# Cross attention: the context tile turned and split earlier in each step

## What is computed

```python
Q = (x @ Wq.T).reshape(B, xN, 16, 32)
KV = (z @ Wkv.T).reshape(B, zN, 2, 16, 32)
K = KV[:, :, 0]
V = KV[:, :, 1]
attn = jnp.einsum('bqhd,bkhd->bhqk', Q, K) * SCALE
attn = jax.nn.softmax(attn, axis=-1)
O = jnp.einsum('bhqk,bkhd->bqhd', attn, V).reshape(B, xN, 512)
return O @ Wo.T
```

## Time and profile before

| | |
|---|---|
| runs | 1499.83, 1495.79, 1500.88 us |
| median | 1499.83 us |
| span of the profiled execution | 1492.9 us |
| PE, PEld busy | 96%, 86% |
| DVE, ACT, POOL busy | 73%, 54%, 36% |

### The profile page before, as it was taken

The page is one execution under the profiler, slowest core; times in us unless marked ns, Lnnn a source line. Parts: engine busy times, 40 slices in busy tenths (PEclk is TensorE's granted clock), DMA queues, the critical chain, the costliest instruction groups (busy, mean ns, idle before and its releaser), DMA issues. The chain is left out here.

```text
span 1492.9 us, 39481 instructions
## 1 busy us (share of the span) xinstructions
PE 1434.5 (96%) x14944; PEld 1281.3 (86%) x14944; DVE 1088.6 (73%) x1945; ACT 807.5 (54%) x1525; POOL 543.6 (36%) x810
## 2 busy tenths in 40 slices
PE   7999999999999999998999998799999999999998
PEld 6888888988888888887778786698999999999997
DVE  3676777767777677776667686797887878787785
ACT  4666666666666666654434434345555545555452
POOL 1222222221222222224866876453333333333232
PEclk9999999999999999999999999899999999999999
DMA  6301101000001100100011014179877878787871
GB/s 239 125 28 31 30 22 29 29 22 29 22 28 28 29 28 23 30 9 1 31 38 38 32 38 155 57 220 314 281 263 247 286 253 267 262 279 238 292 256 44
DMA packets 130734, 174.11 MB, mean 117 GB/s; under 512 B 16953, under 2 KB 89337, under 8 KB 130626
## 3 DMA queue, kind: packets, MB, share of 16 engines
q1 hardware_dynamic: 120242, 145.56, 30.1%
q0 software_dynamic: 10384, 27.05, 5.0%
HBM read 157.18 MB, written 19.06 MB: 118 GB/s over the span
## 5 line engine op out<-in xcount | busy, mean ns | idle before, releaser
L2229 DVE TENSOR_TENSOR split<-raw,split 128x1024 fp32r<-128x1024 f32 x204 | 242.3, 1220 | 7.2 <-ACT split L2169 6.0
L52 PE MATMUL bank<-split_xT,split 128*128 128x256 f32 x768 | 216.5, 282 | 0.4 <-DVE split L2229 0.2
L54 PE MATMUL bank<-split_xT,split 128*128 128x256 f32 x768 | 215.4, 281 | 0.0
L53 PE MATMUL bank<-split_xT,split 128*128 128x256 f32 x768 | 215.4, 280 | 0.0
L2169 ACT CAST split<-raw 128x1024 fp32r<-128x1024 f32 x202 | 203.2, 1048 | 6.9 <-DMA raw<-in_L_ffn_W_dram 3.2
L596 ACT ACTIVATE Pr<-xa_s,nmax 128x257 f32<-128x257 f32 x256 | 118.7, 473 | 124.9 <-DVE nmax L696 124.8
L2189 ACT ACTIVATE sl<-bank 128x256 f32<-128x256 f32 x115 | 44.2, 384 | 240.8 <-PE bank L54 223.5
L52 PE MATMUL xa_s<-split,split 128*128 128x258 f32 x512 | 150.5, 294 | 1.9 <-DVE split L628 1.9
L52 PEld LDWEIGHTS bank<-split_xT,split 128*128 128x128 f32 x768 | 144.9, 189 | 7.0 <-issue 2.8
L53 PEld LDWEIGHTS bank<-split_xT,split 128*128 128x128 f32 x768 | 145.0, 189 | 3.1
L53 PE MATMUL xa_s<-split,split 128*128 128x258 f32 x512 | 145.6, 284 | 0.0
(11 more groups left out here) (317 smaller groups left out, 3915.1 us busy)
## 6 DMA issues: line engine op xcount, KB each, us to landing
raw<-in_L_ffn_W_dram SPq DMA_DIRECT2D x207, 512.0 KB
raw<-in_ctx_dram SPq DMA_DIRECT2D x64, 256.0 KB, 2.6
out_dram<-x_res SPq DMA_DIRECT2D x16, 256.0 KB
xs<-xn SPq DMA_DIRECT2D x16, 256.0 KB
x_res<-in_x_dram SPq DMA_DIRECT2D x1, 3584.0 KB, 18.7
VL<-v_last_rows SPq DMA_DIRECT2D x128, 2.0 KB, 1.5
raw_o<-in_L_xattn_Wo_dram SPq DMA_DIRECT2D x1, 1024.0 KB, 6.4
raw_q<-in_L_xattn_Wq_dram SPq DMA_DIRECT2D x1, 1024.0 KB, 9.5
```

Source lines behind the costliest of these rows:

```text
L52: pe.matmul(out, lh, rh, start=start, stop=False)
L53: pe.matmul(out, ll, rh, start=False, stop=False)
L54: return pe.matmul(out, lh, rl, start=False, stop=stop)
L2229: vW.done(dve.tensor_tensor(lo, raw, hi.bitcast(F32), ALU.subtract), f"p{c}{q}")
```

## The change

Three calls move, one on each of three engines, and nothing is added or removed. On PE `turn_z` of the next step stands right behind the scores (and behind `turn_last`), ahead of the gather. On ACT `z_hi` stands between the second and the third exponential. On DVE `z_lo` stands behind the second maximum (and `last_rows`, `normalise`), ahead of the reciprocal.

```diff
                             turn_last(i - 1)
+                        if not (last and j == BT - 1):
+                            turn_z(s + 1, (j + 1) % BT, i + (j + 1) // BT)
                         if first and j == 1:
                             pe.wait_ge(vl_split, 2)
...
                             turn_x(pe, i + 2)
-                        if not (last and j == BT - 1):
-                            turn_z(s + 1, (j + 1) % BT, i + (j + 1) // BT)
...
                         for m in range(NQ):
+                            if m == 2 and not (last and j == BT - 1):
+                                z_hi(s + 1)
                             act.wait_ge(v_mx, 2 * s + m // 2 + 1)
...
                             x_out(act, i + 2)
-                        if not (last and j == BT - 1):
-                            z_hi(s + 1)
...
                             normalise(dve, i + 2)
+                        if not (last and j == BT - 1):
+                            z_lo(s + 1)
                         dve.wait_ge(a_E, 4 * s + 4)
                         dve.reciprocal(rinv[:], rsum[:]).then_inc(v_R, 1)
...
                             qk_lo(s + 1, u if j < BT - 1 else 1 - u, (j + 1) % BT)
-                            z_lo(s + 1)
```

## The result

| | kernel before | changed kernel |
|---|---|---|
| median of 20 runs each | 1497.1 us (1492.4 to 1500.9) | 1500.95 us (1497.7 to 1504.0) |
| ratio | | 1.0025, 95% interval 1.0016 to 1.0034 |
| span of the profiled execution | 1492.9 us | 1500.4 us |

The change costs 3.8 us where -0.1 was forecast. The median of the kernel before is 2.7 us lower here than in the three runs shown ahead of the prediction. The 1501 us of the changed kernel lie inside the range, and 0.25% is inside the 0.3% that had the chance of 0.77, but only because both were wide: the loss is clear of the measurement, and in the loop, where it begins, I had put it at none. The prediction was wrong.

The account below looks back on a forecast made before the run. PE's own chain was taken to bound the kernel. The terms -0.4 - 0.4 - 0.1 + 0.2 + 0.6 + 0 in the loop gave -0.1 us, a median of 1499.7 us, with the range 1495.0 to 1504.0.

Parts of the forecast that it names:

- the cost of the transposes' move: PE: the gather starts 0.44 us later and ends where the four transposes ended before, sum zero.
- the border before `absorb_k`: PE at j = 0: a 512-wide matmul now precedes absorb_k; taken as nothing, with ends of -1.4 and +1.0 us.
- the delays of the exponentials: ACT: z_hi delays the third exponential 0.2 us at j = 1, 3 and step 0, and costs 0.48 us at j = 0, 2.
- the reciprocal 0.5 us late: DVE at j = 0: z_lo behind last_rows sets the reciprocal 0.51 us late, and the copy of U with it.
- QK's copies don't profit: ACT at j = 0 and 2: copies of QK wait for absorb_k anyway, so PE's 11.8 us of weight loads stay.
- the waits for `z_lo` that go: Three steps in tiles 0, 14 and 15 where the scores wait for z_lo gain 0.4, 0.4 and 0.1 us.
- the first tile: Tile 0: 0.4 us gained at j = 1, 0.2 us lost in step 0, where absorb_k waits for the exponentials.
- my upper end: Border at j = 0: absorb_k waits for the wide matmul's last result, 0.07 us more in 15 steps, 1.0 us.
- All of the loop's 14 steps of this kind come out at zero, with 0.05 us to spare.: Loop at j = 0: values starts 0.18 us late, hidden in the 0.23 us PE waits for QK at turn_p.
- My own sign of being wrong: A tile in the loop changes by more than 0.2 us, most likely by values waiting for U beyond what is hidden.
- the last two tiles: Gains of 0.4 us (tile 14, j = 3) and 0.1 (tile 15, j = 2), loss of 0.6 (tile 15, j = 0).
- I looked for it in the first tile alone: First tile's half clock, 39 to 46 us: lasting once more as long costs about 2.8 us, not occurring gives some 2.5.

Follow-up runs that it names:

- e2: Changed kernel with the old order of transposes, high half and low half at j = 0, the change kept at j = 1 to 3: 1496.2 us, 0.9996 of the kernel before.
- e8: Changed kernel plus a useless second DVE pass over the transposed z at j = 0, ahead of the reciprocal: 1508.1 us, 1.0068 of the kernel before.
- filled kernels: Both kernels plus 9, 3, 6 and 4 useless matmul calls in PE's last-two-tile waits; first session: changed 1494.3 us (0.9971), before 1492.8 us (0.9965).
- e16: Changed kernel with the old order in its last two tiles, the change kept in tiles 0 to 13: 1498.9 us, 1.0022 of the kernel before.
- e11: Kernel before with only PE's transposes moved right behind the scores, plus the smaller fill in the last two tiles: 1492.3 us, 0.9980 of the kernel before.

## Why the prediction was wrong

**Right.** That PE is the bound, with next to nothing for the change to take; the cost of the transposes' move (zero; the border before `absorb_k` too, which starts 6.98 us behind the scores before and 6.95 after); the delays of the exponentials, 0.2 and 0.48 us; the reciprocal 0.5 us late; that QK's copies don't profit; the waits for `z_lo` that go; and the first tile, where -0.4 + 0.2 = -0.2 us was forecast: its four steps took 39.58 and 39.59 us in the two profiles of the kernel before whose clock fell at 39 us, and 39.42 in that of the changed kernel.

The Trainium skill, "TensorEngine Tiling (Array Packing)", Key Properties, has a change of the tiling mode drain TensorE. The traces agree with a hole there, but not with my upper end, by which `absorb_k` would wait for the last result: behind the 512-column matmul `absorb_k` starts 0.55 us after the first of the two, where two take 0.47, so the hole is 0.08 us, like the 0.09 behind the transposes. (The upper end would have put the sum 1.0 us up, to +0.9; "0.9 us up" was a slip.)

**Wrong: "All of the loop's 14 steps of this kind come out at zero, with 0.05 us to spare."** It held in the odd tiles (11.05 us to 11.02) and in tile 2. The five tiles behind the loop's jump were not read; they had 0.31 us less to spare, and 0.22 to 0.29 us a step came through. That is 1.2 us; tile 14 adds 0.1, and with what the other steps gain or lose, 0.03 us or less each, it is 1.1. My own sign of being wrong was there: a tile of the loop that changes by more than 0.2 us, by `values` waiting for U. Undone alone (e2) it goes, doubled (e8) it grows at once: shown.

**Wrong in size: the last two tiles.** Forecast -0.4 in tile 14 and, in tile 15, +0.6 at j = 0 and -0.1 at j = 2, together +0.1; at full clock -0.3, +0.8 and nothing, together +0.5. What was gained at tile 14 didn't carry over: behind its `pt_lo` DVE makes the last key's weights, and those ran into POOL (below), so the maxima of tile 15 weren't earlier. Loop and last tiles give the 1.5 us by which the traces of the filled kernels differ, twice, and that is the loss that is settled.

**Not seen: the clock in the last tiles.** The one profile that I read had full clock there, so I looked for it in the first tile alone. Each of the three profiles of the changed kernel had a stretch of half clock between 600 and 690 us, and one of three of the kernel before. The mean of the stretch in the table of traces is 3.6 us longer with the change, of which 2.1 are this clock. That the fall is tied to PE's waits is shown: of the ten profiles without a fill eight had it, of the eight with one none.

That the change meets it *more often* rests on the granted clock of all runs: 0.0010 and 0.0016 lower than that of the kernel before, which by 1.0 us for 0.001 is an estimate of 1.0 to 1.6 us. With the settled loss this gives 2.5 to 3.1 us, near the 3.1 to 3.8 by which the medians of the unfilled kernels differ. Why it meets it more often is open. The loop's delay is a candidate: the kernel with that delay and the old last pair (e16) has the low clock as well, and the one without it (e2) has not. But e2 had the half clock in its profile, and each of the two was measured on one chip only. And this clock is a mean over the whole span, so it doesn't say in which stage it was low.

By the ratios the unfilled pair differs by 0.25, 0.20 and 0.17%, the filled one by 0.06 and 0.12% (by medians 1.5 and 2.5 us), and each of these is uncertain by 0.1 or more. So 1.5 of the 3.8 us have a settled cause, and the clock accounts for 1 to 2 more as an estimate; the rest is within what two measurements of one kernel differ by.

Neither kernel is the fastest that was run. The kernel before with the small fill lies at 0.9965 and 0.9977 of it in two sessions.

## What to carry to other kernels

A wait that is hidden with 0.05 us to spare must be read in every variant of the step that the code has; a loop that is unrolled by two has two of each, and the one behind the jump may be later, as it was by 0.3 us here. Before moving work ahead of a chain, list who waits for the chain's end in each variant, and subtract. And one profile is one draw of the clock: where PE has stretches of waiting, take two or three before counting the clock as full, and compare the granted clock of all runs. Matmuls of no use in such a stretch can be worth more than the change under study, if they fit in it.

## What the hardware did that I had not expected

DVE's small cast of the last key's probabilities takes 0.17 us in the fourteen tiles in which POOL is idle beside it. At tile 14's end POOL's subtraction for `split_z` runs beside it, and there it takes 0.20 us in the kernel before and 0.78 in the changed one. Timelines, kernel before, DVE, then POOL:

```profile
638.38 0.20 DVE L657 CAST pl_hi<-p_last 128x16 fp32r<-128x16 f32 x1
```

```profile
637.26 1.30 POOL L751 TENSOR_TENSOR split_xT<-raw,split_xT 128x512 fp32r<-128x512 f32 x1
```

The changed kernel, DVE, then POOL:

```profile
640.21 0.78 DVE L657 CAST pl_hi<-p_last 128x16 fp32r<-128x16 f32 x1
641.02 0.18 DVE L659 TENSOR_TENSOR pl_lo<-p_last,pl_hi 128x16 fp32r<-128x16 f32 x1
```

```profile
639.67 1.29 POOL L752 TENSOR_TENSOR split_xT<-raw,split_xT 128x512 fp32r<-128x512 f32 x1
```

It starts 1.13 us into POOL's instruction in the first and 0.54 in the second, and in both ends 0.03 us behind POOL's end; the next DVE instruction has its usual 0.17 or 0.18. With PE's part alone (e11) it starts 0.81 us in, takes 0.51, and ends 0.03 us behind POOL again; in all 18 profiles it ends 0.03 or 0.04 us behind. So this cast ends when POOL's instruction has ended, wherever in it it starts. That holds for this pair of instructions: `pt_lo`, which reads the scores' banks, takes 0.67 to 0.69 us with POOL beside it and without.
